# Two 9x9 adaptive blurs: the order of work in a row of blocks, and the hidden layer on two row tiles

## The reference

```python
h = relu(einsum('bchw,co->bohw', x, w1) + b1)             # 16 channels -> 32 hidden
ks = relu(einsum('bohw,o->bhw', h, w2[:, 0]) + b2) * 20 + 1
sigma = ks / 3
logits = -gauss_kernel / (2 * sigma ** 2)                 # 81 taps for every pixel
wgt = exp(logits); wgt = wgt / sum(wgt)
low = sum over the 81 taps of x_shifted * wgt             # padded with zeros
enhanced = x + low
return (enhanced - mean) / sqrt(var + 1e-5)               # per image and channel
```

## Time and profile before

| | value |
|---|---|
| times of three runs | 534.25, 536.21, 538.63 us |
| the profiled execution: time / its span in the profile | 538.64 / 536.4 us |
| busy TensorE / its weight loads | 412.3 us (77%) / 292.8 us |
| busy VectorE | 340.5 us (63%) |
| busy ScalarE | 268.7 us (50%) |
| busy GpSimd | 181.5 us (34%) |
| first blur (L1) | about 211 to 346 us |
| second blur (L3), with the output | about 390 us to the end |
| HBM traffic over the span | 45 GB/s |

### The profile page before, as it was taken

One profiled execution on the slowest core, in us unless ns is written; L12 is line 12 of the kernel. 1 busy time (PEld: TensorE's weight loads), 2 busy tenths in 40 slices (PEclk: granted clock), 3 DMA queues, 4 the chain that ended last, 5 costly groups with the idle time before them and its releaser, 6 DMA issues. The chain is left out here.

```text
span 536.4 us, 15849 instructions
## 1 busy us (share of the span) xinstructions
PE 412.3 (77%) x7024; PEld 292.8 (55%) x7024; DVE 340.5 (63%) x525; ACT 268.7 (50%) x298; POOL 181.5 (34%) x118
## 2 busy tenths in 40 slices
PE   4487988878999198668887886499965888887871
PEld 1177923217989122436665675377743466666760
DVE  2794586745888965336676786648433367777683
ACT  1665585653333000346787877411016386788581
POOL 3220022320000002137776794000030777777700
PEclk9879999997999789878999999879978799999897
DMA  8930000000000000022222220000000232332003
GB/s 188 187 138 1 1 1 1 0 1 1 2 2 3 1 0 0 2 79 83 83 82 82 84 81 4 3 1 0 0 1 25 96 122 83 82 83 82 4 4 156
DMA packets 17055, 24.83 MB, mean 46 GB/s; under 512 B 6735, under 2 KB 8544, under 8 KB 16864
## 3 DMA queue, kind: packets, MB, share of 16 engines
q1 hardware_dynamic: 15968, 23.52, 14.8%
q10 hardware_dynamic: 1024, 0.36, 0.4%
HBM read 21.53 MB, written 2.34 MB: 45 GB/s over the span
## 5 line engine op out<-in xcount | busy, mean ns | idle before, releaser
L1240 POOL TENSOR_TENSOR g_wgt<-g_exponents,g_s_wide 128x1024 f32<-128x1024 f32 x56 | 131.9, 2380 | 67.8 <-PE ps L977 34.0
L1083 ACT ACTIVATE g_wgt<-g_wgt 128x2048 f32<-128x2048 f32 x64 | 121.1, 1908 | 24.1 <-DVE g_wgt L1145 24.1
L977 PE MATMUL ps<-g_wgt,g_xt 128*32 128x64 f32 x4096 | 74.9, 224 | 25.3 <-issue 17.5
L977 PEld LDWEIGHTS ps<-g_wgt,g_xt 128*32 128x32 f32 x4096 | 63.9, 112 | 44.1 <-issue 31.5
L1145 DVE TENSOR_TENSOR g_wgt<-g_exponents,ps 128x1024 f32<-128x1024 f32 x72 | 84.9, 1202 | 2.6 <-PE ps L963 2.6
L1056 ACT ACTIVATE g_hid<-ps,vec 128x512 f32<-128x512 f32 x32 | 20.3, 684 | 85.2 <-PE ps L925 85.2
L1153 DVE COPY g_num<-ps 128x512 f32<-128x512 f32 x32 | 22.0, 688 | 56.0 <-PE ps L977 55.9
L963 PE MATMUL ps<-ident,g_scl 128*128 128x128 f32 x288 | 46.7, 302 | 4.0 <-DVE g_wgt L1145 2.7
L963 PEld LDWEIGHTS ps<-ident,g_scl 128*128 128x128 f32 x288 | 35.1, 151 | 9.0 <-DVE g_wgt L1145 4.0
L469 PE MATMUL ps<-conv_img,projblk 128*32 128x512 f32 x256 | 35.8, 681 | 0.0
L1439 PE MATMUL ps<-high,wb 128*128 128x512 f32 x72 | 30.5, 424 | 5.3 <-DVE rest L1468 5.3
(11 more groups left out here) (169 smaller groups left out, 731.1 us busy)
## 6 DMA issues: line engine op xcount, KB each, us to landing
g_s_wide<-g_s_rows SPq DMA_DIRECT2D x56, 256.0 KB, 3.7
x<-in_x SPq DMA_DIRECT2D x8, 256.0 KB, 6.9
x<-in_x SPq DMA_DIRECT2D x1, 2048.0 KB, 8.7
out<-g_result SPq DMA_DIRECT2D x4, 512.0 KB, 3.9
windows<-band SPq DMA_DIRECT2D x4, 256.0 KB, 5.3
g_s_rows<-g_srow SPq DMA_DIRECT2D x56, 4.0 KB
c_weight<-in_c_weight SPq DMA_DIRECT2D x1, 576.0 KB, 4.2
g_w<-in_g_w SPq DMA_DIRECT2D x2, 128.0 KB, 2.7
```

The lines of the kernel that those rows point to most:

```text
L977: mm = pe.matmul(ps[32 * j:32 * j + 32, O_BANK, 64 * cb:64 * cb + 64], xt[(s + t) % 2][:, cb, b, :], weights_of(s, b)[:, t, cb, :], start= ...
L1083: act.activation(w, w, ACT.Exp).then_inc(weight, 1)
L1240: pool.tensor_tensor(weights_of(s, b), spread(gband[:].unsqueeze(2), shape), spread(s_wide[s][j][:].unsqueeze(1), shape), ALU.mult).then_i ...
```

## The change

**The order of the work.** `pe_row(r)` now does both sums of row r. While they run, ScalarE's and VectorE's row r makes the products and exponentials of row r+1. What was made in `*_first_row` is now in `*_begin`: all products of row 0, and its exponentials, come before the first sum, and the small layers of rows 0 to 2 too. `hidden(1)` now stands ahead of `xt(0)`, and `hidden(2)` ahead of `xt(1)`. `enhance(r)` and `stats(r)` move into VectorE's row r+1, with one of each behind the last row. ScalarE's order of pairs is 0, 1, 2, 3 with pair 3 last, behind `xt`.

**The hidden layer on two row tiles.** Each of the two matmuls of `hidden` reads only the 64 partitions of its images, weights and pixels: the first partitions 0 to 63 into bank 7, the second 64 to 127 into bank 6. They use the upper and the lower half of the array's rows.

**Waits.** `hidden(r)` waits for `scale(r-1)` and, from r = 2, for `xt_out` of r-1. `ks_turn(r)` waits for `xt_out` of r. `xt(g)` waits for `relu(g+1)`.

The core of the diff:

```diff
     def pe_hidden(pe, r):
-        if r == 1 or r == 2:
-            pe.wait_ge(xt_out, r)
-        elif r > 2:
+        if r >= 1:
+            pe.wait_ge(small, 3 * r)
+        if r >= 2:
             pe.wait_ge(xt_out, r - 1)
-            pe.wait_ge(small, 3 * r)
-        rows = slice(BLK * r + R, BLK * r + R + BLK)
         for i, bank in enumerate((MLP_BANK, XT_BANK)):
-            mm = pe.matmul(ps[:, bank, :], w1[:, i, :], pad[:, rows, R:R + W], start=True, stop=True)
+            planes = slice(64 * i, 64 * i + 64)
+            mm = pe.matmul(ps[:, bank, :], w1[planes, i, :], pad[planes, BLK * r + R:BLK * r + R + BLK, R:R + W],
+                           start=True, stop=True)
         mm.then_inc(hid_mm, 1)
...
     def pe_ks_turn(pe, r, s):
         pe.wait_ge(small, 3 * r + 2)
+        if r >= 1:
+            pe.wait_ge(xt_out, r)
...
     def pe_xt(pe, g, s):
-        pe.wait_ge(small, 3 * g + 3 if g < 2 else min(3 * g + 6, 3 * RB))
+        pe.wait_ge(small, min(3 * g + 4, 3 * RB))
...
+    def pe_begin(pe):
+        pe_hidden(pe, 0)
+        pe_ks(pe, 0)
+        pe_ks_turn(pe, 0, 0)
+        for v in range(4):
+            pe_spread(pe, 0, 0, v)
+        pe_hidden(pe, 1)
+        pe_ks(pe, 1)
+        pe_xt(pe, 0, 0)
         pe_spread(pe, 0, 0, 4)
+        pe_ks_turn(pe, 1, 1)
         pe_spread(pe, 0, 0, 5)
         pe_spread(pe, 0, 0, 6)
+        pe_hidden(pe, 2)
+        pe_ks(pe, 2)
         pe_spread(pe, 0, 0, 7)
         pe_xt(pe, 1, 1)
+        for v in range(3):
+            pe_spread(pe, 1, 1, v)
...
     def act_row(act, r, s):
+        if r + 1 < RB:
+            act_weight(act, r + 1, 1 - s, 0)
         if r + 3 < RB:
             act_hidden(act, r + 3)
+        if r + 1 < RB:
+            act_weight(act, r + 1, 1 - s, 1)
+            act_weight(act, r + 1, 1 - s, 2)
+        if r + 3 < RB:
+            act_square(act, r + 3)
+        if r + 2 <= RB:
+            act_xt(act, r + 2, s)
+        if r + 3 <= RB:
+            act_stage(act, r + 3, 1 - s)
+        if r + 1 < RB:
+            act_weight(act, r + 1, 1 - s, 3)
...
     def dve_row(dve, r, s):
+        if r + 1 < RB:
+            dve_logit(dve, r + 1, 1 - s, 0)
+        if r >= 1:
+            dve_enhance(dve, r - 1)
+        if r + 1 < RB:
+            dve_logit(dve, r + 1, 1 - s, 1)
         if r + 2 < RB:
             dve_scale(dve, r + 2, s)
+        dve_num(dve, r, 0)
+        if r + 1 < RB:
+            dve_logit(dve, r + 1, 1 - s, 2)
+        dve_mix(dve, r, 0)
+        if r >= 1:
+            dve_stats(dve, r - 1)
+        if r + 1 < RB:
+            dve_logit(dve, r + 1, 1 - s, 3)
+        dve_num(dve, r, 1)
+        if r + 3 < RB:
+            dve_relu(dve, r + 3)
+        dve_mix(dve, r, 1)
+        if r + 3 < RB:
+            dve_inverse(dve, r + 3, 1 - s)
```

More of the change, by code:

```diff
@@ L1046, in pe_row @@
         if r + 3 < RB:
-            pe_ks(pe, r + 3)
+            pe_hidden(pe, r + 3)
+        pe_turn(pe, r, 0)
+        if r + 2 < RB:
+            pe_spread(pe, r + 2, s, 0)
+        pe_blur(pe, r, s, 1, 0)
+        pe_blur(pe, r, s, 1, 1)
+        if r + 3 < RB:
+            pe_ks(pe, r + 3)
+        if r + 2 < RB:
+            pe_spread(pe, r + 2, s, 1)
+        pe_turn(pe, r, 1)
+        if r + 2 <= RB:
+            pe_xt(pe, r + 2, s)
+        if r + 2 < RB:
+            pe_spread(pe, r + 2, s, 2)
+        pe_low(pe, r)
     def act_hidden(act, r):
@@ L1176, in dve_stats, with dve_begin @@
                      pad[:, slice(BLK * r + R, BLK * r + R + BLK), R:R + W]).then_inc(stat, 1)
-    def dve_first_row(dve):
+    def dve_begin(dve):
         dve_logit(dve, 0, 0, 0)
+        dve_relu(dve, 1)
         dve_logit(dve, 0, 0, 1)
-        dve_relu(dve, 1)
+        dve_inverse(dve, 1, 1)
         dve_logit(dve, 0, 0, 2)
-        dve_inverse(dve, 1, 1)
+        dve_scale(dve, 1, 1)
         dve_logit(dve, 0, 0, 3)
-        dve_scale(dve, 1, 1)
+        dve_relu(dve, 2)
         dve_logit(dve, 0, 0, 4)
-        dve_relu(dve, 2)
-        dve_logit(dve, 0, 0, 5)
         dve_inverse(dve, 2, 0)
[L1190 to L1193, removed]
+        for v in range(5, B):
+            dve_logit(dve, 0, 0, v)
     def dve_row(dve, r, s):
-        if r + 2 < RB:
-            dve_relu(dve, r + 2)
-        if r < RB:
-            dve_logit(dve, r, s, 0)
-        if r + 2 < RB:
-            dve_inverse(dve, r + 2, s)
-        if r < RB:
-            dve_logit(dve, r, s, 1)
+        if r + 1 < RB:
[4 more added lines that the diff above has]
+            dve_logit(dve, r + 1, 1 - s, 1)
         if r + 2 < RB:
             dve_scale(dve, r + 2, s)
-        dve_mix(dve, r - 1, 0)
-        dve_num(dve, r - 1, 1)
-        if r < RB:
-            dve_logit(dve, r, s, 2)
-            dve_logit(dve, r, s, 3)
-        dve_mix(dve, r - 1, 1)
-        if r < RB:
-            dve_num(dve, r, 0)
-        dve_enhance(dve, r - 1)
-        dve_stats(dve, r - 1)
+        dve_num(dve, r, 0)
[10 more added lines that the diff above has]
+        dve_mix(dve, r, 1)
+        if r + 3 < RB:
+            dve_inverse(dve, r + 3, 1 - s)
     def half_tile(g, s, odd):
@@ L1293, in _ @@
                 pe.wait_ge(a, 16)
-            pe_hidden(pe, 0)
-            pe_ks(pe, 0)
-            pe_ks_turn(pe, 0, 0)
-            for v in range(4):
-                pe_spread(pe, 0, 0, v)
-            pe_xt(pe, 0, 0)
-            pe_hidden(pe, 1)
-            pe_ks(pe, 1)
+            pe_begin(pe)
             pe.wait_ge(const_ready, 4)
-            pe_first_row(pe)
-            for r in range(1, RB + 1):
+            for r in range(RB):
                 pe_row(pe, r, r % 2)
@@ L1309, in _ @@
             act.wait_ge(band_ready, 1)
-            act_hidden(act, 0)
-            act_square(act, 0)
-            act_xt(act, 0, 0)
-            act_hidden(act, 1)
-            act_first_row(act)
-            for r in range(1, RB):
+            act_begin(act)
+            for r in range(RB):
                 act_row(act, r, r % 2)
@@ L1341, in _ @@
             dve.wait_ge(band_ready, 2)
-            dve_first_row(dve)
-            for r in range(1, RB + 1):
+            dve_begin(dve)
+            for r in range(RB):
                 dve_row(dve, r, r % 2)
+            dve_enhance(dve, RB - 1)
+            dve_stats(dve, RB - 1)
             dve.wait_ge(stat, RB)
```

56 lines of the change are left out of this document (11 added, 45 removed).

## The result

| kernel | median of its runs, us | ratio to the kernel before, 95% interval |
|---|---|---|
| before, on the same chip | 536.64 (534.25 to 538.63, 4 runs) | 1 |
| changed | 518.71 (516.19 to 522.16, 4 runs) | 0.967 (0.960 to 0.975) |

What follows compares the result with a forecast made beforehand. No engine was full; a loop of waits crossing twice from TensorE to ScalarE set 13.2 us a row. Savings of 12.3 + 13.1 + 9 + 10 + 1.4 = 45.8 off the 536.21 median gave 491 us, range 480 to 507.

Steps and rivals of the forecast that it cites:

- the term of the halts: TensorE's stops in the middle of a group, with no releaser, during the eight rows: kept at 5.0 us a blur.
- 45.8 promised: Total saving in us: 12.3 and 13.1 in the rows, 9 and 10 before them, 1.4 behind them.
- my 71.1: Forecast us between the copies of sum 0 in row 0 and row 7 of a blur, without TensorE's halts.
- the beginnings: From the first `hidden` to sum 0's copy in row 0: 9 us saved in the first blur, 10 in the second.
- The ends: Behind row 7's first sum, the second no longer waits for an exponential: 0.7 us saved a blur.
- The loop and its length: Middle rows: TensorE's row up to `xt`, ScalarE's copy, then the next first sum; 10.52 us instead of 13.2.
- The second crossing: Middle rows: TensorE's second wait on ScalarE, for row r's exponentials, leaves the loop because they are made a row earlier.
- The row tiles: The two matmuls of `hidden` run side by side: 0.95 us instead of 1.81; not side by side, 504 us, chance 0.12.
- The drain at a change of mode: Around `hidden`: at most 0.07 us a change, 0.05 added a row; rival by the skill's rule 495 us, chance 0.14.
- The alternating waits of TensorE and VectorE: Rival: four of a row's eight handoffs miss by 0.35 us, a row takes 11.9, 506 us; chance 0.10.
- the halts grow: Rival: transfers squeezed into 10.5 us rows lengthen TensorE's stops until the kernel is slower, 540 to 550 us; chance 0.03.
- The wait only moves: Rival: `hidden` is late for ScalarE, with pairs 1 and 2 behind it; 517 us, chance 0.04.

Runs made afterwards that it cites:

- order alone: The changed kernel with the hidden layer on all 128 partitions again, no row tiles; 521.74 us, ratio 0.972 to the kernel before.
- small loads: The changed kernel, but from row 3 on each SyncE load of `s_wide` writes one partition instead of 128; 508.15 us, ratio 0.940.
- half of the taps: The changed kernel with half the matmuls of every sum left out, loads as they are; 484.69 us, ratio 0.904.

## Why the prediction was wrong

**The step that failed** is the term of the halts: "Other lines have a few, so I keep 5.0 a blur, as now." They measured 13.9 and 13.7. I treated them as a constant of the kernel, since the profile names no releaser for them. They belong to the resource that the change leans on. A row has some 630 instructions for TensorE, two and a half pieces of 256. In the kernel before, a part of a sum (128 instructions in 1.03 us) had something slower behind it, and a row lasted 13.2 us. The change puts two parts together, 256 instructions in 1.92 us, and wants the row in 10.5. In the two blurs a piece begins 2.2 us or more behind the start of its packet, never earlier, the packet starts only after the piece before has begun, and where that one lasts about 2 us TensorE stops at its end, and often at the end of the next.

**The account.** 45.8 promised, 21.7 found, so 24.1 are missing:
- 17.5 are halts beyond the 10.0 kept (27.5).
- 4.8 more are in rows 0 to 7: 86.1 - 13.9 = 72.2 and 88.4 - 13.7 = 74.8, against my 71.1. In the second blur about 2.8 of its 3.7 are TensorE's clock behind a halt. Windows view, changed kernel (length, busy time by engine, then TensorE's granted clock as a share):

```profile
450.00:453.00 3.00, 3.00 (x13) 1.31 (x12) 1.65 (x2) 0.54 (x1) 3.00 (x3) 0.64 0.55 173
469.00:472.00 3.00, 3.00 (x17) 3.00 (x16) 1.55 (x4) 0.40 (x1) 3.00 (x2) 0.53 0.00 0
```

  The clock was 1.00 in the clean row before, and falls to its lower level, 1.2 GHz, behind the halts of 2.01 and 2.46 us, and behind the one of 3.04 in the first blur; behind those of 2.09 and 2.00 it stayed at 2.4. `hidden` and `xt` then take twice their time (timeline):

```profile
450.48 1.93 PE L924 MATMUL ps<-pad_b,g_w 64*128 64x512 f32 x4
...
468.61 0.42 PE L934 MATMUL ps<-g_hid,g_w 128*32 128x128 f32 x5 [2.46 <-issue]
...
470.52 1.91 PE L953 MATMUL ps<-ident,g_tile 128*128 128x128 f32 x8
```

  The longest row of the second blur, 16.4 us from the copy of sum 0 at 461.52 to the one at 477.92, is 10.6 + 2.46 + 1.67 of halts + 1.7 for the clock.
- 1.8 are the beginnings: 7.7 and 9.5 saved, not 9 and 10.
- The ends gave 1.5, as said (1.4).

**What held, step by step:**
- *The loop and its length.* The second crossing is gone and the row without its halt is 10.58, against 10.52. Answering to the earlier trace rows, the windows view of the row from 432.45, changed kernel:

```profile
432.45:444.79 12.34, 10.30 (x314) 8.44 (x315) 9.54 (x16) 10.43 (x10) 5.58 (x4) 1.00 0.31 90
```

  TensorE's 10.30 busy, the 0.28 ahead of the first sum and the halt of 1.76 make up the 12.34. VectorE's and ScalarE's work is what I took.
- *The row tiles.* `hidden` goes from 1.81 to 1.06 from start to start (435.08 to 436.14), against my 0.95; its records span 1.13 instead of 1.88. The two tiles run side by side: the four records start in pairs, at 435.08 and 435.09, and at 435.61 and 435.62. The 0.11 more are 1 to 2 us in all.
- *The drain at a change of mode.* The spread ahead of `hidden` takes 0.53 from start to start (434.55 to 435.08), the same as the one ahead of the second sum (436.63 to 437.16), where the mode changes too. With the order alone, `hidden` has the mode of its neighbours, and the spread ahead of it takes 0.45 (timeline, order alone):

```profile
459.45 0.60 PE L964 MATMUL ps<-ident,g_scl 128*128 128x128 f32 x4
459.90 1.98 PE L923 MATMUL ps<-pad_b,g_w 128*128 128x512 f32 x4
```

  So the change ahead of `hidden` costs 0.08, near the 0.07 that I had as the most; the 0.05 that I added for both was low. The Trainium skill, TensorEngine Tiling (Array Packing), section Tiling Modes, has the drain as a property of a mode change. The trace agrees, and the price is small.
- *The beginning.* `relu(1)` of the second blur starts 13.8 us behind the first `hidden` (379.55), against 13, and sum 0's copy 30.1 behind it, against 28.6 to 30.4 (timeline, VectorE):

```profile
393.31 0.35 DVE L1130 TENSOR_SCALAR g_relu<-ps,vec 128x128 f32<-128x128 f32 x1 [4.92 <-PE ps L934]
...
409.62 0.68 DVE L1162 COPY g_num<-ps 128x512 f32<-128x512 f32 x1
```

- *The alternating waits of TensorE and VectorE.* `turn` waited for the copies 4.0 us in the second blur's rows, 6 times, and 3.1 of it in rows 6 and 7, where the forecast had such waits. It is not what lengthened the rows.

**The rivals.** The one that happened is the one I gave 0.03: the halts grow. I priced it only from the point at which it eats the whole gain, and so it stood in the range as nothing or as everything. In between, with some 40% of the gain eaten, is where the kernel is. I argued against it with the transfers alone ("now fill 13.2 us, fall in 10.5"), and that is the smaller part: 27.5 us of halts against 20.0 with the small ones. The rival *The wait only moves* gives 517 us, near the 518.71, by chance: `hidden` did not slip, and the row without its halt was 10.58.

**What stays open.** Shown is where TensorE stops (at the end of 256 instructions), that it needs dense instructions (none with half of the taps), and that loads in a burst make it worse. The trace also shows what the loads do. From the start of the packet to the end of the halt are 2.2 to 2.9 us at each of the 150 halts, with whole loads and with small ones; what differs is when the packet starts. In 29 pieces of the two blurs it started 2.2 us on the mean behind the beginning of the piece before it in the changed kernel, and 1.7 with small loads; for the halt that ends at 468.61 it was 2.5 us, against 0.1 with small loads. That the request stands behind the loads in that time is argued, since the request itself is not in the trace. Not shown is the rule by which a packet is asked for: its start bears no fixed distance to the beginning of the piece before (438.64 against 437.21, but 446.12 against 441.12), and it was 4.6 us late at the latter place with small loads too. It lies between 1.4 us ahead of the time when TensorE runs dry and 0.7 behind it. The Trainium skill, Advanced Engine Details and Errata, section ISA Cache, gives lines of 16 KB or 256 instructions, which these runs bear out, and 128 KB of them on TensorE. No run here shows a reserve of that size: at the halts, TensorE had nothing left beyond the piece in hand.

## What to carry to other kernels

An idle time in the middle of a group of like instructions, with no releaser, is not noise: count the instructions between two of them, and if the count repeats, the engine waits for its own program, and more instructions in less time will bring more of it. When a change packs the smallest and quickest instructions of an engine closer together, charge it for the reading of them (here 256 at a time, and 2.2 to 2.9 us from the start of the packet until the engine resumes), and look for loads that can be spread out: one wait on SyncE gave back half as much again as the change had brought. A price that the profile shows but does not explain belongs in the range with its middle values, and not only with the one at which it decides.

## What the runs showed of the hardware

- TensorE's instructions come in packets of 16 KB, 256 instructions, on a DMA queue that the page lists as q8: 53 of them in the whole kernel, 37 with 4096 instructions fewer, and 54 with 285 more.
- A halt ends 2.2 to 2.9 us behind the start of its packet, in every kernel here, whether the loads of data are whole or small; the halts themselves last up to 3.1 us. Loads in a burst make the packet start later, not last longer until the halt ends.
- All 150 halts stand at the same remainder of 256 by the trace's count of TensorE's instructions, wherever in the program that falls.
- Behind three of the changed kernel's five halts of 2 us or more (2.01, 2.46 and 3.04) the granted clock fell to its lower level, with means of 0.64 and 0.53 over 3 us behind the first two, in stretches where TensorE was busy without a pause; behind the other two (2.00 and 2.09) it did not.
- An instruction that only waits, for a semaphore long given, takes TensorE's queue 0.106 us where many stand in a row.
- A change from tiles of 128 rows to tiles of 64 costs about 0.08 us (0.53 us for the spread ahead of `hidden`, against 0.45 without the change).
- Two matmuls of 512 columns on the upper and the lower half of the array's rows take 1.06 us together, against 1.81 for two on the whole array.
